# Expert rows and shared rows added to the output in memory by accumulating scatters, in an adaLN block with a mixture of experts

## The reference, cut to what matters

```python
mod = (_silu(L0_c) @ L0_wmod).reshape(4, 6, 1, -1)      # sa, ca, ga, sb, cb, gb for each of 4 sequences
ga = (2 * (ga >= 0) - 1) * jnp.maximum(jnp.abs(ga), 0.25)   # gb likewise
h = _layernorm(x, axis=-1) * (1 + ca) + sa
x = x + ga * _L0_attn_ref(h, w_qkv, w_proj, b_proj)     # relu(q), relu(k), key-value sums over 1024 tokens
h = _layernorm(x, axis=-1) * (1 + cb) + sb
# experts: top 2 of 8 by sigmoid score, y_e = (silu(h W1_e) * (h W3_e)) W2_e, inner width 352
# shared: (silu(h sw1) * (h sw3)) sw2, inner width 704
x = x + gb * (sum over the 2 experts of weight * y_e + shared)
```

## Time and profile before

| what | value |
|---|---|
| median of 3 runs | 1335.45 us |
| the profiled execution | 1328.03 us |
| its span in the trace | 1326.3 us |
| TensorE busy | 1229.3 us, 93% of the span |
| VectorE, ScalarE, POOL busy | 664.9, 413.8, 396.9 us |
| mean granted TensorE clock | 0.976 |
| DMA | 219.08 MB, 165 GB/s |

### The profile page before, as it was taken

The page is one execution under the profiler, slowest core; times in us unless marked ns, Lnnn a source line. Parts: engine busy times, 40 slices in busy tenths (PEclk is TensorE's granted clock), DMA queues, the critical chain, the costliest instruction groups (busy, mean ns, idle before and its releaser), DMA issues.

```text
span 1326.3 us, 25206 instructions
## 1 busy us (share of the span) xinstructions
PE 1229.3 (93%) x9054; PEld 781.5 (59%) x9054; DVE 664.9 (50%) x1382; ACT 413.8 (31%) x869; POOL 396.9 (30%) x367
## 2 busy tenths in 40 slices
PE   6998998998997998977896999999999999989998
PEld 2645665665565665654564565656656665657675
DVE  6455877867777666577884211111111111126465
ACT  4332444433443332423333122222222222212121
POOL 2112656655654433200001011111111111056552
PEclk9998999999999999988998999999999999989999
DMA  7714687898896865733444455555565565489986
GB/s 233 210 42 128 165 192 191 197 219 167 206 214 162 235 184 166 233 124 112 139 146 129 112 130 133 142 123 141 135 129 137 128 141 130 111 224 239 253 232 173
DMA packets 269204, 219.08 MB, mean 165 GB/s; under 512 B 188496, under 2 KB 200784, under 8 KB 268572
## 3 DMA queue, kind: packets, MB, share of 16 engines
q1 hardware_dynamic: 239832, 155.31, 45.7%
q0 software_dynamic: 12848, 35.40, 12.0%
q10 hardware_dynamic: 16408, 26.77, 6.4%
HBM read 116.69 MB, written 56.94 MB: 131 GB/s over the span
## 4 chain that ended last, share of the span: by engine, by line
PE 51%; DVE 15%; POOL 10%; DMA 10%; issue 8%; ACT 3%; SPq 2%; ACTq 1%; DVEq 0%; POOLq 0%
PE ps_o L86 6%; PE ps_o L88 6%; PE ps_o L87 6%; PE ps_vs L86 5%; PE ps_vs L87 5%; PE ps_vs L88 5%; DMA xt<-g 3%; DMA wp_raw<-in_wproj_t 2%; PE ps_vh L86 2%; PE ps_vh L88 2%; PE ps_vh L87 2%; POOL ol L412 2%; DVE w_all L682 2%; POOL h L388 2%; POOL h L399 2%
## 5 line engine op out<-in xcount | busy, mean ns | idle before, releaser
L471 POOL DMA_INDIRECT g<-h_d,slot_token x71 | 67.8, 956 | 507.1 <-DMA xt<-g 350.0
L86 PE MATMUL ps_o<-w_all,xt 128*128 x568 | 178.7, 315 | 11.6 <-DMA xt<-g 11.6
L88 PE MATMUL ps_o<-w_all,xt 128*128 x568 | 178.6, 315 | 0.0
L87 PE MATMUL ps_o<-w_all,xt 128*128 x568 | 178.6, 314 | 0.0
L914 DVE TENSOR_TENSOR at<-ps_y,at 128x384 f16<-128x384 f32 x71 | 39.6, 558 | 176.5 <-ACT at L1171 176.5
L909 DVE SCALAR_TENSOR_TENSOR a<-ps_o,a 128x352 f32<-128x352 f32 x71 | 37.3, 525 | 173.1 <-PE ps_o L88 173.1
L1176 ACT ACTIVATE y<-ps_vs,slot_weight 128x512 f32<-128x512 f32 x71 | 48.8, 688 | 230.6 <-PE ps_vs L88 230.6
L86 PE MATMUL ps_qh<-ht,wqkv 128*128 128x128 f16 x512 | 88.9, 221 | 8.3 <-DVE qt L549 4.9
L88 PE MATMUL ps_qh<-ht,wqkv 128*128 128x128 f16 x512 | 88.9, 221 | 0.0
L87 PE MATMUL ps_qh<-ht,wqkv 128*128 128x128 f16 x512 | 88.9, 221 | 0.0
L86 PE MATMUL ps_kh<-s_ht,sh 128*128 128x256 f16 x256 | 71.3, 278 | 12.4 <-DMA s_ht<-h2t_d 8.9
(11 more groups left out here) (240 smaller groups left out, 3179.6 us busy)
## 6 DMA issues: line engine op xcount, KB each, us to landing
y_d<-y SPq DMA_DIRECT2D x71, 256.0 KB, 3.5
w_stage<-in_w_d ACTq DMA_DIRECT2D x64, 176.0 KB, 2.5
xb<-in_x SPq DMA_DIRECT2D x32, 256.0 KB, 3.5
xr<-in_x SPq DMA_DIRECT2D x32, 256.0 KB, 3.7
x_d<-x SPq DMA_DIRECT2D x32, 256.0 KB, 3.4
h_d<-hl SPq DMA_DIRECT2D x32, 256.0 KB, 2.6
h2t_d<-h2t SPq DMA_DIRECT2D x32, 256.0 KB, 3.4
s_xs<-x_d SPq DMA_DIRECT2D x32, 256.0 KB
```

The costliest lines, as they stand in the source:

```text
L86: nc.tensor.matmul(out, lh, rh, start=first, stop=False, skip_group_check=True)
L87: nc.tensor.matmul(out, lh, rl, start=False, stop=False, skip_group_check=True)
L88: return nc.tensor.matmul(out, ll, rh, start=False, stop=last, skip_group_check=True)
L471: pool.indirect_dma_start(m.g[:, t % 2, :], None, m.h2_d, bass.IndirectOffsetOnAxis(ap=m.slot_token[:, t:t + 1], axis=0)).then_inc(m.gathe ...
```

## The change: what it does

The shared expert's 96 steps all run before the experts, and the experts' 71 tiles come last. x2 is stored straight to `out`, which gets 128 spare rows at its end. The shared rows, times gb, are added to `out` by an accumulating indirect DMA (32 of them, POOL). Each expert tile's rows are multiplied on VectorE by the slot's weight and by the gb row of its token, which a second gather brings (71 gathers from gb_d, 4 rows), and are added to `out` by an accumulating scatter (71 of them), one after the other. Slots without a token go to the spare rows. Gone are: the store of y, `fetch`, `fetch_onto` and `combine`, the reload of x2 and the store of x2s. The ring of gathered and of transposed tiles goes from 2 to 4. Conversion of weights: 12 pieces in the slots, 76 over steps 24 to 89; the masks: one token tile to a step. LAG goes from 8 to 9, so there are 44 slots, 12 of them with shared steps. The high half of the key-value sums goes to ScalarE, the sums are made by 4 VectorE instructions where there were 8. The modulation rows 2 to 5 are made transposed: 64 float32 matmuls with 4 columns, clamped on 128 partitions, turned back by one transpose.

```diff
-LAG = BT
+LAG = BT + 1
-EARLY_STEPS = SH_TILES * EARLY
+EARLY_STEPS = SH_TILES * CHUNKS
+G_RING, GB_RING, Y_RING = 4, 3, 3
...
 def w_turn(q):
     if q < TAIL_STEPS:
-        return range(q, q + 1)
+        return range(q // 2, q // 2 + 1) if q % 2 else range(0)
...
+        return spread(TAIL_PIECES, E * WP, q - TAIL_STEPS, EARLY_STEPS - LAST_PIECES - TAIL_STEPS)
...
-            sp.dma_start(rows_of(m.x2_d, t), m.x2[:, t % X2_RING, :]).then_inc(m.x2_stored[t % X2_RING], 16)
+            sp.dma_start(rows_of(m.out, t), m.x2[:, t % X2_RING, :]).then_inc(m.x2_stored[t % X2_RING], 16)
...
     def turn_g(t):
         if t < SLOT_TILES:
-            sp.wait_ge(m.gathered[t % 2], ring_use(t, 2))
-            at_least(sp, m.h3_done, t - 1)
-            sp.dma_start_transpose(m.xt[:, t % 2, :, :], m.g[:, t % 2, :]).then_inc(m.xt_loaded[t % 2], 16)
+            if t == 2:
+                sp.wait_ge(m.up_done, EARLY_STEPS - SH_TILES)
+            sp.wait_ge(m.gathered[t % G_RING], ring_use(t, G_RING))
+            at_least(sp, m.h3_done, t - G_RING + 1)
+            sp.dma_start_transpose(m.xt[t % G_RING][:, :, :], m.g[t % G_RING][:, :]).then_inc(m.xt_loaded[t % G_RING], 16)
...
+    def add_shared(n):
+        for u in range(2):
+            t = 2 * n + u
+            pool.wait_ge(m.s_t1_done, t + 1)
+            pool.wait_ge(m.x2_stored[t % X2_RING], ring_use(t, X2_RING))
+            pool.indirect_dma_start(m.out, bass.IndirectOffsetOnAxis(ap=m.row_no[:, t:t + 1], axis=0), m.s_sum[:, u, :], None,
+                                    compute_op=ALU.add).then_inc(m.shared_added[u], 16)
...
+    def gather_gate(t):
+        if t < SLOT_TILES:
+            r = t % GB_RING
+            at_least(pool, m.ey_ready, t - GB_RING + 1)
+            pool.indirect_dma_start(m.gbr[r][:, :], None, m.gb_d,
+                                    bass.IndirectOffsetOnAxis(ap=m.slot_batch[:, t:t + 1], axis=0)).then_inc(m.gbr_loaded[r], 16)
+
+    def scatter(t):
+        pool.wait_ge(m.ey_ready, t + 1)
+        at_least(pool, m.scattered, 16 * t)
+        pool.indirect_dma_start(m.out, bass.IndirectOffsetOnAxis(ap=m.slot_row[:, t:t + 1], axis=0), m.y[:, t % Y_RING, :], None,
+                                compute_op=ALU.add).then_inc(m.scattered, 16)
...
+    gather(2)
+    gather(3)
+    gather_gate(1)
+    gather_gate(2)
+    add_shared(CHUNKS - 1)
+    pool.wait_ge(m.spare_stored, 16)
+    for j in range(2):
+        pool.wait_ge(m.shared_added[j], 16 * CHUNKS)
     for t in range(SLOT_TILES):
-        gather(t)
...
+        scatter(t)
+        gather(t + G_RING)
+        gather_gate(t + GB_RING)
+    pool.wait_ge(m.scattered, 16 * SLOT_TILES)
...
+            at_least(v, m.shared_added[u], 16 * n)
+            v.scalar_tensor_tensor(out=m.s_sum[:, u, :], in0=m.ps_sy[u][:, 0:C], scalar=1.0 / SCALE, in1=m.s_gb[:, (t // BT) % 2, :],
+                                   op0=ALU.mult, op1=ALU.mult).then_inc(m.s_t1_done, 1)
...
+    def e_out(t):
+        r = t % GB_RING
+        v.wait_ge(m.ey_done, t + 1)
+        v.wait_ge(m.gbr_loaded[r], ring_use(t, GB_RING))
+        at_least(v, m.scattered, 16 * (t - Y_RING + 1))
+        v.scalar_tensor_tensor(out=m.y[:, t % Y_RING, :], in0=m.ps_ey[:, 0:C], scalar=m.slot_weight[:, t:t + 1], in1=m.gbr[r][:, :],
+                               op0=ALU.mult, op1=ALU.mult).then_inc(m.ey_ready, 1)
...
+        for row, j in ((GA, 2), (GB, 5), (SHIFT, 3), (GAIN, 4)):
+            for c in range(KC):
+                for k in range(KC):
+                    at = j * C + c * P
+                    mm = nc.tensor.matmul(m.ps_modt[:, row, :, c], m.wmod[:, k, at:at + P], m.sct[:, k, :], start=k == 0, stop=k == KC - 1)
...
-            pe.wait_ge(m.s_t1_done, 2 * EARLY)
+            pe.wait_ge(m.s_t1_done, 2 * CHUNKS)
         e_down(t - 1)
     e_turn(SLOT_TILES - 1)
-    for q in range(EARLY_STEPS, SH_TILES * CHUNKS):
...
+    e_down(SLOT_TILES - 1)
```

More of the change, by code:

```diff
@@ L114, in w_turn @@
     if q < TAIL_STEPS:
-        return range(q, q + 1)
-    if q <= LIST_STEP:
-        return spread(TAIL_STEPS, SHARED_PIECES, q - TAIL_STEPS, LIST_STEP + 1 - TAIL_STEPS)
+        return range(q // 2, q // 2 + 1) if q % 2 else range(0)
     if q < EARLY_STEPS - LAST_PIECES:
-        return spread(SHARED_PIECES, E * WP, q - LIST_STEP - 1, EARLY_STEPS - LAST_PIECES - LIST_STEP - 1)
+        return spread(TAIL_PIECES, E * WP, q - TAIL_STEPS, EARLY_STEPS - LAST_PIECES - TAIL_STEPS)
     return range(0)
 def down_due(q):
-    return q >= SH_TILES and q % SH_TILES == 0 and q // SH_TILES != EARLY
+    return q >= SH_TILES and q % SH_TILES == 0
 def add_due(q):
-    return q >= SH_TILES and q % SH_TILES == 1 and q // SH_TILES != EARLY
+    return q >= SH_TILES and q % SH_TILES == 1
 def list_turn(q):
-    first = TURNS_PER_STEP * (q - TURNS_FROM)
-    return range(first, first + TURNS_PER_STEP) if 0 <= first < TILES else range(0)
+    return range(q - TURNS_FROM, q - TURNS_FROM + 1) if tile(q - TURNS_FROM) else range(0)
 def step_width(j):
     return P if j < SH_TILES - 1 else SH_HALF
[L140 to L153, removed]
 def sync_program(nc, m, sp):
@@ L450, in gpsimd_program @@
         deviation2(t - 1)
+        if s >= TILES:
+            for q in range(STEPS_PER_SLOT * (s - TILES), STEPS_PER_SLOT * (s - TILES + 1)):
+                if add_due(q):
+                    add_shared(q // SH_TILES - 1)
     pool.wait_ge(m.scores_ready, 1)
@@ L492, in fetch_onto @@
-    def fetch_onto(i):
-        r = i % YB
-        pool.wait_ge(m.y_loaded[i % Y_RING], 2 * ring_use(i, Y_RING) - 16)
-        pool.indirect_dma_start(m.yb[:, r, 0, :], None, m.y_d,
-                                bass.IndirectOffsetOnAxis(ap=m.slot[:, 1, order[i]:order[i] + 1], axis=0),
-                                compute_op=ALU.add).then_inc(m.y_loaded[i % Y_RING], 16)
-    for i in range(3):
-        fetch(i)
-    for i in range(len(order)):
-        fetch_onto(i)
-        fetch(i + 3)
+    gather(0)
@@ L508, in vector_program @@
-    place_of = {t: i for i, t in enumerate(order)}
     def stats(i):
@@ L732, in vector_program @@
             multiply(q)
+            divide(t)
             low(q - 1)
@@ L1105, in scalar_program @@
             split_high(n)
+            if s == -1 and n < 9:
+                load_stage(n + 3)
         if s == -2:
@@ L1585, in place_buffers @@
     m.passed = sb("passed", [1, SLOT_TILES, E], F32)
-    sb = region(W_STAGE_AT, W_AT)
-    m.g = sb("g", [P, 2, 2 * C], F16)
-    m.xt = sb("xt", [P, 2, 2 * KC, P], F16)
+    GATE_AT, ACT_AT, AT_AT, T1_AT = SHARED_AT + 8192, SHARED_AT + 12288, SHARED_AT + 14336, SHARED_AT + 24576
+    first, second, third = region(W_STAGE_AT, W_AT), region(SHARED_AT + 4096, GATE_AT), region(SHARED_AT, SHARED_AT + 4096)
+    m.g = [(first, first, second, second)[j](f"g{j}", [P, 2 * C], F16) for j in range(G_RING)]
+    m.xt = [(first, first, third, third)[j](f"xt{j}", [P, 2 * KC, P], F16) for j in range(G_RING)]
+    m.gbr = [region(at, at + 2048)(f"gbr{j}", [P, C], F32) for j, at in enumerate((GATE_AT, ACT_AT, T1_AT))]
+    m.y = region(AT_AT, AT_AT + 6144)("y", [P, Y_RING, C], F32)
     sb = region(W_END, END)
```

446 lines of the change are left out of this document (170 added, 276 removed).

## The result

The changed kernel takes **1367.9 us** (median of 4 runs, 1364.6 to 1372.7), the kernel before 1334.9 us in 4 runs on the same chip: ratio 1.025, 95% interval 1.021 to 1.030. The forecast was 1296 us, range 1262 to 1342, and 71% for faster. The time lies outside the range, on the other side. The profiled execution has a span of 1371.0 us, 45 us more than before.

What follows compares the result with a forecast made beforehand. TensorE, busy 93% of 1326.3 us, was taken as the bound. 1326.3 less 33, 7 and 12, plus 20 lost among the experts, gave a 1294 us span and a forecast of 1296 us, range 1262 to 1342.

Steps and rivals of the forecast that it cites:

- Part 1: Lone shared steps moved ahead of the experts: of 38 us lost there, 33 us come back.
- Rival 3: Shared stage keeps its stalls: half the 38 us stay, tiles take 6.3 us, 1320 us in all; chance 10%.
- Part 2: Last stage: 17 us over its 42 steps, 10 us remain behind the last expert matmul, 7 us back.
- Part 3: Attention and its slots: sequence-start stalls 7 us, earlier first shared input 5 us, together 12 us back.
- Modulation: Modulation rows: 64 transposed products cost 9 to 18 us against 14 for four rows; taken as 0, 5 either side.
- The shared rows' scatters: In the slots: two scatters of about 1.9 us per chunk on POOL, costing nothing to little.
- rival 1: Expert stage: no loop binds, landings stay and tiles take 5.85 us, 1271 us in all; chance 22%.
- Part 4: Expert stage: two loops through POOL and memory raise a tile from 5.85 to 6.2 us; 20 us lost net.
- The chain of scatters: Expert stage: scatter(t+1) waits until scatter(t) has landed; placed at 6.0 to 6.5 us.
- D: Expert stage: a scatter's time from issue to landing, setting the tile time if scatters bind; no change at 6.65 us.
- The loop of gather and transpose: Expert stage: gather(t+4) stands behind scatter(t) on POOL; 10.8 us against 11.7, landings 1.5 to 2 us longer.
- Rival 2: Expert stage: each scatter waiting for the last sets the pace, 1367 us at 7.2 us from issue to landing; chance 17%.

Runs made afterwards that it cites:

- plain scatters: Changed kernel with the experts' 71 scatters writing instead of adding, so the sum is left out; 1285.1 us.
- gather first: Changed kernel with POOL issuing the gather of tile t+4 ahead of the scatter of tile t; 1334.6 us.
- plain shared scatters: Changed kernel with the 32 scatters of the shared rows writing instead of adding, so x2 is lost from those rows; 1357.5 us.
- two-target: Changed kernel with odd tiles' scatters going to a second buffer, each waiting for the one before the last; 1371.6 us.
- both loops: Changed kernel with the gather ahead of the scatter and odd tiles' scatters to a second buffer; 1301.1 us.

## Why the prediction was wrong

**Part 1, right.** 33 us were to come back from the lone shared steps. The stretch has 11 idle us in 282. By the prediction's own count 282.5 us (565 to 847.5) are 72 steps of 3.7 (266), the list matmuls (8) and 8 over, where 38 were over: 30 came back. Chunks with list matmuls take 24.3 us and later ones 22.16 (ScalarE, same step of two chunks: 771.00 and 793.16), as the earlier trace rows has it, and the waits for masks are down to 2.2 us from 10.2:

```profile
771.00 0.38 ACT L957 ACTIVATE s_act<-ps_kh 128x256 f32<-128x256 f32 x1 [1.55 <-PE ps_kh L89]
...
793.16 0.38 ACT L957 ACTIVATE s_act<-ps_kh 128x256 f32<-128x256 f32 x1 [1.42 <-PE ps_kh L89]
```

The clock came out at 1.00, as said. Rival 3 fell. Wrong in it was only that the first expert tile would start without a wait: TensorE waits 6.1 us for it, as before.

**Part 2, right in its size as far as can be seen:** from the last `y` (1360.51) to the end of the span are 10.5 us, 10 were counted.

**Part 3, half right.** The stalls at the starts of sequences are 2.1 us where they were 8.8, but the same product now waits 5.2 us for VectorE's `v_sb` where it waited 1.8. In place of the 8.9 us for the first shared input stand 2.2 us, but another product of the slots (line 1192, the router's logits) now waits 7.8 us, for no releaser that the profile shows. Modulation at 0 with 5 to either side was 22.7 us against 14 before, 9 us; the bound of 18 was broken because it took the weight load at the full clock. The shared rows' scatters at "nothing to little" cost up to 10 us. With plain scatters of the experts the kernel takes 1285 us against the 1271 of rival 1: 14 us is what parts 1 to 3 were off together, and modulation and these scatters cover it.

**Part 4 failed,** in the sentence "both loops ask for 6.1 to 6.5. I take 6.2 us a tile": the chain was taken too low, and the two loops were priced apart, as if the slower one alone set the pace. Its two halves:

- *The chain of scatters* was put in the right place and then taken too low. The trace of the kernel before had more to say than the 6.0 and 7.2 us that were read from it: POOL waited 19 times for an accumulating fetch of the last stage, with turns of 5.2 to 8.9 us and a median of 6.7, so 7.2, the longest row shown, was not the longest there was. This one was, POOL in order of time (from the issue of the fetch to the next issue that waited for it, 8.9 us):

```profile
1180.59 1.55 POOL L495 DMA_INDIRECT yb<-y_d,slot  x1 [0.30 <-issue]
...
1189.52 0.97 POOL L489 DMA_INDIRECT yb<-y_d,slot  x1 [3.66 <-DMA yb<-y_d,slot]
```

  In the changed kernels the turn measured 6.3 to 6.5 us as a median, inside the 6.0 to 6.5 that the text had from the earlier trace rows; a chain of 71 such turns costs 71 x 0.6 = 44 us, not 25. The kernel with the gather first shows it alone: 6.47 us a tile and 1334.6 us, the whole gain gone. The prediction put that point at D = 6.65; the 14 us by which parts 1 to 3 were off move it by 14/71 = 0.2 us, to 6.45.
- *The loop of gather and transpose* was right in its landings, or nearly, and lacked a wait. The landings were to come 1.5 to 2 us longer together; in the kernel with plain shared scatters, which has the same expert stage, they are 5.5 and 5.0 us at the median where they were 3.8 and 4.3, 2.4 us more. By the prediction's own rule that alone is (10.8 + 2.4) / 2 = 6.6 us a tile. But it counted scatter(t) as issued as soon as `y` was there. POOL waited 44.5 us for the scatter before, and VectorE 15.6 us for the place of `y` that a scatter holds, in 870 to 1355 us: 0.9 us a tile, inside this loop, since the gather stands behind that scatter. With it, (10.8 + 2.4 + 0.9) / 2 = 7.05, an estimate from means; 7.05 was measured. That the waits themselves are part of the loop is what the two-target and gather-first kernels bear out together. The gather behind the scatter costs (7.05 - 6.47) x 71 = 41 us against the order gather first; 33 were measured.

Together: 1296, and 19 for the chain (6.47 for 6.2), 41 for the gather's place, 9 for modulation, 3 over: 1368. The 41 come from the profiled run, which took 1372.7 us, 5 above the median. The parts overlap, so the sum is a reading and no proof; shown are the 83 us of the addition, the 33 of the order, and the 67 of both loops.

**Rival 2** had the time (1367 us) at D = 7.2 by luck, not by the mechanism: scatters turned in 6.4 us, and the missing 0.6 us a tile came from the other loop, which starts its gathers when a late scatter lets it. Two loops that each looked 0.3 us over a tile met in one in-order queue: a scatter that waits delays the gather behind it, a late tile delays `y`, and `y` the next scatter. The chance of 17% was too low, since the nearest operation had turns with a median of 6.7 us, above 5.85 like both that the earlier trace rows show, and the 4.4 that held the range open came from an operation that adds nothing. The engine load, 72 to 89 engine-us of 93.6, was about right (0.80 x 16 x 7.05 = 90) and not what decided: shares of 0.69 and 0.71 went with 6.50 and 6.22 us a tile, 0.86 with 5.87.

The Trainium skill (DMA: Bandwidth & Descriptors, Anatomy of one DMA, SWDGE path) gave an estimate of 4.2 us with the issue. The lowest median landings of an accumulating 256 KB scatter are 4.7 us, for the shared rows, and 4.8 for the experts' beside gathers alone; beside transposes they were 5.2 to 5.7. The fixed part and the bytes of the Trainium skill make no difference between writing and adding, and here a writing scatter of the shared rows landed in 3.0 us. The remark of the Trainium skill (same page, Latency and other measured facts) that an access to HBM takes longer under high load fits the direction of the 0.7 us that the transposes made, but the landings did not follow the DMA share.

**Open:** whether the transposes lengthen a scatter by 0.7 us as such or by their traffic; why tiles of the same expert stage took 6.84, 6.89 and 7.05 us; which of the adding transfer's parts (reading, the addition, writing) is long; the wait of 7.8 us at line 1192.

## What to carry to other kernels

Before transfers that must follow one another are put into a loop, compare the whole turn (issue, landing, restart of the queue's engine) of the nearest like transfer with the loop's period: if it is above, the chain is the bound, whatever the mean load of the DMA engines, and splitting it into independent chains of smaller transfers opened it here. In an in-order queue, put what feeds the next work ahead of what waits for the last. When two loops pass through one queue, add the wait of the one to the sum of the other; they do not take turns at being the bound. If a loop's slack is under 1 us while every landing in it is about to share memory with new traffic, give the slower side its chance.

## What the runs showed of the hardware

- An accumulating scatter of 128 rows of 2 KB into memory: issued by POOL in 1.60 us (a writing one in 0.98), landed 4.8 us after the start of its issue beside gathers, 5.2 to 5.7 beside gathers and transposes (medians), some 28 to 36 engine-us of DMA where a writing one takes 13. For the shared rows adding landed in 4.7 us and writing in 3.0. The restart behind a landed one is 0.75 to 0.8 us. Two halves of the columns in parallel chains gave 5.87 us a tile where one whole gave 6.42, at a DMA share of 0.86 against 0.71.
- TensorE's granted clock fell from 1.00 to 0.50 (2.4 to 1.2 GHz) within a gapless run of matmuls of 4 columns (59.7 to 82.4 us) and stayed there to its end; TensorE was busy in the profile all the while. A product pass took 0.10 us before and 0.20 behind. It fell too within a tile behind a wait of 4 us, and cost up to 20 us in the expert stage of the changed kernel; in the versions with few such waits it stands at 1.00.
- A DMA share above 1 was seen (1.05 at 5.97 us a tile) with TensorE idle for 6 of 370 us: a share near 1 is no proof that the engines are the bound.
